# One attention body of a recurrent block: state products in strips, variances in float32r, key gates behind the first values

## The reference

```python
gk = jax.nn.log_sigmoid(xn @ Wkg1 @ Wkg2 + bkg2) / NORMALIZER
v = xn @ Wv
g = xn @ Wg + bg
def step(S, inp):
    qt, kt, vt, gt = inp
    S = S * jnp.exp(gt)[..., None] + kt[..., None] * vt[..., None, :]
    ot = jnp.einsum('bhk,bhkd->bhd', qt, S)
    return (S, ot)
mu = jnp.mean(o, axis=-1, keepdims=True)
var = jnp.var(o, axis=-1, keepdims=True)
o = (o - mu) * jax.lax.rsqrt(var + 1e-05)
o = jax.nn.silu(g) * o
x = x + o @ Wo
```

## Time and profile before

| | us |
|---|---|
| runs: lowest, median, highest | 1624.19, 1628.15, 1628.93 |
| profiled execution: its own time, span | 1622.4, 1620.7 |
| PE busy | 1593.2 (98%) |
| PE weight loads busy | 1277.6 (79%) |
| DVE busy | 847.3 (52%) |
| ACT busy | 567.2 (35%) |
| POOL busy | 167.2 (10%) |

### The profile page before, as it was taken

How to read it: one execution, slowest core, us unless ns; L and a number is a source line. 1 busy time by engine, 2 the same in 40 slices (tenths; PEclk the granted TensorE clock), 3 DMA queues, 4 the chain that set the end, 5 groups by cost and what they waited for, 6 DMA issues and landing times.

```text
span 1620.7 us, 30581 instructions
## 1 busy us (share of the span) xinstructions
PE 1593.2 (98%) x12274; PEld 1277.6 (79%) x12274; DVE 847.3 (52%) x1311; ACT 567.2 (35%) x982; POOL 167.2 (10%) x190
## 2 busy tenths in 40 slices
PE   7999999999999999999999999999999999999998
PEld 5777888777777777777777788888888888888886
DVE  5565455367797887978876451331415142241413
ACT  4333343366564645636564411111111111111111
POOL 4770000100220102101020000000000000000000
PEclk9999999999999999999999999999999999999999
DMA  7563332101020210202213423030301203030200
GB/s 175 151 135 78 83 95 69 59 27 52 9 84 0 84 53 32 84 0 84 84 54 118 144 101 127 0 136 0 136 0 49 87 0 136 0 136 0 91 14 26
DMA packets 50700, 113.16 MB, mean 70 GB/s; under 512 B 13321, under 2 KB 24665, under 8 KB 42466
## 3 DMA queue, kind: packets, MB, share of 16 engines
q1 hardware_dynamic: 47906, 99.95, 19.5%
q10 hardware_dynamic: 1152, 8.39, 1.3%
q0 software_dynamic: 1600, 4.25, 0.9%
HBM read 78.98 MB, written 33.59 MB: 69 GB/s over the span
## 4 chain that ended last, share of the span: by engine, by line
PE 94%; DVE 2%; ACT 1%; issue 1%; DMA 1%; PEld 0%; SPq 0%; ACTq 0%; DVEq 0%; PEldq 0%
PE m_ps L1529 10%; PE m_ps L1531 10%; PE m_ps L1530 10%; PE a_ps L160 7%; PE a_ps L162 7%; PE a_ps L161 7%; PE f_ps L160 5%; PE f_ps L162 5%; PE f_ps L161 5%; PE m_ps L1543 5%; PE m_ps L1544 5%; PE m_ps L1545 5%; PE a_att L1282 3%; PE a_ps L1399 2%; PE a_ps L1303 2%; PE a_ps L1390 1%
## 5 line engine op out<-in xcount | busy, mean ns | idle before, releaser
L1529 PE MATMUL m_ps<-m_xshi,m_w 128*128 128x512 f32 x680 | 268.1, 394 | 1.4 <-DVE m_w L1520 1.4
L1766 DVE TENSOR_TENSOR m_h<-m_ps,m_silu 128x512 f32<-128x512 f32 x85 | 58.7, 690 | 402.4 <-PE m_ps L1531 402.4
L1531 PE MATMUL m_ps<-m_xshi,m_w 128*128 128x512 f32 x680 | 266.5, 392 | 0.0
L1530 PE MATMUL m_ps<-m_xslo,m_w 128*128 128x512 f32 x680 | 266.4, 392 | 0.0
L1830 ACT ACTIVATE m_silu<-m_ps 128x512 f32<-128x512 f32 x85 | 50.8, 597 | 334.3 <-PE m_ps L1531 334.3
L1529 PEld LDWEIGHTS m_ps<-m_xshi,m_w 128*128 128x128 f32 x680 | 127.7, 188 | 30.0 <-issue 2.1
L1531 PEld LDWEIGHTS m_ps<-m_xshi,m_w 128*128 128x128 f32 x680 | 127.6, 188 | 28.7
L1530 PEld LDWEIGHTS m_ps<-m_xslo,m_w 128*128 128x128 f32 x680 | 127.7, 188 | 28.1 <-issue 0.2
L1101 POOL TENSOR_TENSOR row<-row,a_r 128x512 f32<-128x512 f32 x32 | 50.7, 1615 | 331.6 <-DMA a_r<-scratch_r 331.6
L1022 DVE TENSOR_TENSOR a_a<-a_att,causal 128x1024 f32<-128x1024 f32 x64 | 75.2, 1216 | 11.8 <-PE a_att L1282 11.8
L1839 ACT ACTIVATE m_h0hi<-m_h 128x512 fp32r<-128x512 f32 x46 | 29.1, 632 | 135.7 <-DVE m_h L1766 135.7
(11 more groups left out here) (306 smaller groups left out, 3487.9 us busy)
## 6 DMA issues: line engine op xcount, KB each, us to landing
row<-scratch_xn SPq DMA_DIRECT2D x16, 1024.0 KB, 4.9
row<-scratch_xmid SPq DMA_DIRECT2D x16, 1024.0 KB, 7.3
m_xt<-in_L_attn_W SPq DMA_DIRECT2D x33, 256.0 KB, 3.2
f_xt<-in_L_attn_x SPq DMA_DIRECT2D x32, 256.0 KB, 8.1
scratch_xn<-row SPq DMA_DIRECT2D x8, 1024.0 KB, 9.0
scratch_gate<-row ACTq DMA_DIRECT2D x8, 1024.0 KB, 3.9
scratch_xmid<-row SPq DMA_DIRECT2D x8, 1024.0 KB, 3.9
row<-scratch_gate SPq DMA_DIRECT2D x8, 1024.0 KB, 10.5
```

The costliest lines, as they stand in the source:

```text
L1529: pe.matmul(ps, wh, xh, start=k == 0, stop=False)
L1530: pe.matmul(ps, wh, xl, start=False, stop=False)
L1531: ins = pe.matmul(ps, wl, xh, start=False, stop=k == LAST)
L1766: dve.tensor_tensor(h[n], dense.region(f"b{j}"), silu[n], ALU.mult).then_inc(dense.taken_sem(f"b{j}"), 1)
```

## The change

Five edits go together.

1. The state is kept for two heads per strip of 32 partitions (`state`, 64 columns a group instead of 256). The products with the queries become eight strips of 32 rows and 64 columns, and the outputs of a chunk go to two PSUM banks, `ps_mix` EVEN and ODD, half of each.
2. Half of the ODD bank holds the turned keys; when neither is in use the whole of it is the third bank of `dense` (z0, v2, g1, o0, o3). The other results go by turns to the two remaining banks (`places`). v1 and g0 are still neighbours in one bank, as are g0 and g3.
3. ScalarE splits the squares into a high part, VectorE makes the low part (`squares_lo`), and the variance is two float32r products.
4. The inner gate is laid out in four groups of 16 rows, taken out by one copy on ScalarE and one subtraction on VectorE, instead of three copies and a subtraction on VectorE.
5. On TensorE and ScalarE the keys' transposes of chunks 1 and 2 move behind the parts of row i + 1, and z moves behind v0 and the last variance.

```diff
@@ phase_a @@
-        state = [sb(f"state{n}", [P, GR, HG * VH]) for n in range(2)]
+        state = [sb(f"state{n}", [P, GR, 2 * VH]) for n in range(2)]
...
-        psum = [ctx.enter_context(nc.psum_tensor(f"a_ps{b}", [P, 512], F32))[:] for b in range(4)]
+        psum = [ctx.enter_context(nc.psum_tensor(f"a_ps{b}", [P, 512], F32))[:] for b in range(2)]
+        ps_mix = ctx.enter_context(nc.psum_tensor("a_mix", [P, 2, 512], F32))[:]
+        EVEN, ODD = 0, 1
...
+        places = {result: n for n, results in enumerate((
+            ["k0", "ds0", "var0", "q0", "ds2", "var2", "v0", "z1", "v3", "g2", "o1"],
+            ["k1", "u", "ds1", "var1", "q1", "ms", "var3", "v1", "g0", "g3", "o2"],
+            ["z0", "v2", "g1", "o0", "o3"])) for result in results}
...
+        turned = Regions(count, "kt", [ps_mix[:, ODD, GR * P:]], list(range(NC - 1)))
...
@@ vector @@
-                dve.tensor_copy(u[0:RANK], ps).then_inc(count.sem("uhi"), 1)
-                dve.tensor_copy(u[64:64 + RANK], ps).then_inc(count.sem("uhi"), 1)
-                dve.tensor_copy(u[96:96 + RANK], at.region("u")[32:32 + RANK]).then_inc(count.sem("uhi"), 1)
...
+            def squares_lo(i, c):
+                dve.wait_ge(*count.at("sqhi", i, c + 1))
+                dve.tensor_tensor(og_hl[1][:, :, tokens(c)], sq, og_hl[0][:, :, tokens(c)].bitcast(F32),
+                                  ALU.subtract).then_inc(count.sem("sqlo"), 1)
...
@@ scalar, body @@
-                    if c + 1 < NC:
-                        act.wait_ge(*dense.ready(f"kt{c}", i))
-                        act.activation(flat(kt_sb), dense.region(f"kt{c}")[:, 0:GR * P],
-                                                            ACT.Copy).then_inc(dense.taken_sem(f"kt{c}"), 1)
-                    for part in (("k0", "k1"), ("c1",), ("q0",), ("q1",))[c]:
+                    if c == 0:
+                        keys(i, c)
+                    if c == 1:
+                        squares(i, (2,))
+                    for part in (("k0", "k1"), ("u",), ("q0",), ("q1",))[c]:
                         ahead(part)
+                    if 0 < c < NC - 1:
+                        keys(i, c)
...
+                    act.wait_ge(*count.at("sq", i, c + 1))
+                    act.activation(og_hl[0][:, :, tokens(c)], sq, ACT.Copy).then_inc(count.sem("sqhi"), 1)
-                ahead("z")
                 ahead("v0")
                 inverse_deviation(i, NC - 1)
+                ahead("z")
                 ahead("exponentials")
                 ahead("g")
...
@@ tensor @@
-                pe.matmul(ps, avg32, flat(sq), start=True, stop=True).then_inc(dense.ready_sem(f"var{c}"), 1)
+                pe.matmul(ps, avg32r, og_hl[0][:, :, tokens(c)], start=True, stop=False)
+                pe.matmul(ps, avg32r, og_hl[1][:, :, tokens(c)], start=False, stop=True).then_inc(dense.ready_sem(f"var{c}"), 1)
...
-                        for quad in range(QD):
-                            g, first_head = quad * HQ // HG, quad * HQ % HG
-                            pe.matmul(ps[:, quad, :], state[c % 2][:, g, first_head * VH:(first_head + HQ) * VH],
-                                      qhat[:, gcs[g], :], start=quad == 0, stop=True, skip_group_check=True)
+                        for g in range(GR):
+                            for strip in range(4):
+                                rows, at = slice(H32 * strip, H32 * (strip + 1)), H64 * (strip % 2)
+                                pe.matmul(ps[2 * g + strip // 2][at:at + H64], state[c % 2][rows, g, :],
+                                          qhat[rows, gcs[g], :], start=g == 0, stop=True, skip_group_check=True,
+                                          tile_position=(H32 * strip, at))
...
-                ahead("z")
                 ahead("v0")
                 variance(i, NC - 1)
+
+                pe.wait_ge(*mix.taken(NC - 1, i))
+                ahead("z")
                 ahead("v1")
                 ahead("g")
```

More of the change, by code:

```diff
@@ L57, with __init__ @@
 class Regions:
-    def __init__(self, counts, name, regions, order, early=()):
+    def __init__(self, counts, name, regions, order, early=(), places=None):
         self.counts, self.name, self.regions = counts, name, regions
@@ L269, in prepare_attention_weights @@
     step(pool.memset(w["wkg2"].bitcast(F32), 0.0))
-    step(pool.memset(w["wkg1"].bitcast(F32), 0.0))
     RANK, KD = Wkg2.shape
-    small = w["stage"][0:RANK, 1, 0:KD]
+    small = w["stage"][0:4 * RANK, 1, 0:KD]
     sources = {"wkg1": Wkg1, "wk": Wk, "wq": Wq, "wv": Wv, "wg": Wg, "wo": Wo}
@@ L296, in prepare_attention_weights @@
         if name == "wkg1":
-            hi, lo = (w[name][:, kt, at:at + cols] for at in (0, 32))
+            copies = [w[name][:, kt, n * RANK:(n + 1) * RANK] for n in range(4)]
+            for copy in copies[1:3]:
+                step(pool.tensor_copy(copy, s))
+            hi, lo = copies[0], copies[3]
         else:
@@ L843, in phase_a @@
         assert GR == 2 and NC == 4
[L845 to L848, removed]
+        order = [("k0", ["k0"]), ("k1", ["k1"]), (None, ["ds0"]), ("u", ["u"]), (None, ["var0", "ds1"]),
+                 ("q0", ["q0"]), (None, ["var1", "ds2"]), ("q1", ["q1"]), (None, ["var2", "ms"]),
+                 ("v0", values[:1]), (None, ["var3"]), ("z", zs), ("v1", values[1:]), ("g", gates),
                  (None, outs), ("body", [])]
+        places = {result: n for n, results in enumerate((
+            ["k0", "ds0", "var0", "q0", "ds2", "var2", "v0", "z1", "v3", "g2", "o1"],
+            ["k1", "u", "ds1", "var1", "q1", "ms", "var3", "v1", "g0", "g3", "o2"],
+            ["z0", "v2", "g1", "o0", "o3"])) for result in results}
         early = {part: results for part, results in order if part}
-        late = {order[n + 1][0]: results for n, (part, results) in enumerate(order) if not part}
-        dense = Regions(count, "dense", psum[0:3], sum((results for _, results in order), []), sum(early.values(), []))
+        dense = Regions(count, "dense", psum + [ps_mix[:, ODD]], sum((results for _, results in order), []),
+                        sum(early.values(), []), places)
+        turned = Regions(count, "kt", [ps_mix[:, ODD, GR * P:]], list(range(NC - 1)))
         att = Regions(count, "att", ps_att, [f"{c}_{n}" for c in range(NC) for n in range(2)])
-        mix = Regions(count, "mix", psum[3:4], list(range(NC)))
+        mix = Regions(count, "mix", [ps_mix[:, :, 0:QD // 2 * P]], list(range(NC)))
         LAST = KT - 1
+        s_avg = outer.enter_context(nc.semaphore("a_avg"))
         parity, s_parity = sb("parity", [P, 2]), outer.enter_context(nc.semaphore("a_parity"))
@@ L1019, in body @@
                     for n in range(2):
+                        if c > 0 and n == 1:
+                            squares_lo(i, c - 1)
                         dve.wait_ge(*att.ready(f"{c}_{n}", i))
@@ L1379, in body @@
                     pe.wait_ge(*mix.free(c, i))
-                    ps = mix.region(c).rearrange("p (q t) -> p q t", t=P)
+                    ps = [mix.region(c)[:, (EVEN, ODD)[quad % 2], quad // 2 * P:(quad // 2 + 1) * P] for quad in range(QD)]
+                    if 0 < c < NC - 1:
+                        pe.wait_ge(*turned.taken(c, i))
                     if c > 0:
@@ L1433, in tensor @@
             f.tensor(pe, first_row)
-            for part in ("v0", "v1", "g"):
+            parts["v0"](0)
+            pass_over(pe, dense, ["z1"], 0)
+            for m in range(KT):
+                pe.wait_ge(*f.dense.taken(f"u{m}", NB - 1))
+            for part in ("v1", "g"):
                 parts[part](0)
+            pe.wait_ge(s_avg, 1)
             loop_parts(pe, NB, parts, body, skip=front.tensor(pe), first=False)
```

118 lines of the change are left out of this document (65 added, 53 removed).

## The result

The changed kernel takes 1683.88 us (median of four runs, 1682.46 to 1684.81), against 1628.32 for the kernel before on the same chip. That is 55.6 us more, or 1.034 times as long by the two medians; the recorded ratio of the runs is 1.0357, 95% interval 1.0341 to 1.0372. Its profiled execution took 1684.57 us with a span of 1682.8, 62.2 us more than the one before, which lies 5.9 us under the median of its kernel. The forecast was 1651, at most 1664: the direction was right and the size about half.

The account below looks back on a forecast made before the run. TensorE, busy 98% of the span, bounds the kernel. About +3.9 us in each of six steady bodies (+23.4), +5 in body 0 and 0 in body 7 gave +28 on 1622.4: 1651 us, 8 in 10 range 1634 to 1664.

Parts of the forecast that it names:

- the wait and its chain: Before g0: z behind v0 delays absolute values by 3.67 us and v1's copy, so TensorE waits 4.0 us a body.
- M: Moment the last chunk's products of weights and values are done, 599.18 before the change, where the key gate products start.
- the case that the forecast priced at 3.1: Rival at g0: offsets pass ahead of GpSimd's first operation, wait only 3.1 us, 1639 us in all; chance 0.30.
- strips that do not run together: Rival in 24 chunks: strips take 0.98 or 1.96 us instead of 0.49, giving 1663 to 1686 us; chance 0.08.
- Behind it g1 waits for v2's copy and g3 for ScalarE's silu of g0: Output gates after the wait at g0: two further waits that move with the chain, 0.9 us a body together.
- M 1.0 us earlier: Inside the chunks: TensorE savings of 0.63, 0.63 and 0.80 us less 1.1 us of new waits, per body.
- a wait of 0.2 us in chunk 1 for VectorE: Chunk 1: keys' product waits 0.2 us while VectorE empties the inner gate's bank after causal products and squares_lo.
- the 1.1 us of waits that the prediction had in the chunks: New TensorE waits: 0.3 us for keys' copies in chunks 1 and 2 each, 0.2 and 0.3 for banks.
- body 0 and body 7: First and last body: +5 us for body 0; 0 for body 7, its savings of 1.3 eaten by weight copies.
- The forecast's four delays: Body 0: moved sums, scans and offsets fall into GpSimd's 7.87 us; four delays of 1.1 for one, +5 us.

Follow-up runs that it names:

- Experiment 2: Kernel before with only z's products moved behind v0 and the last variance on TensorE and ScalarE: 1677.92 us, 1.0307.
- experiment 5: Changed kernel with GpSimd's scaling of the next row held back until VectorE has computed the offsets: 1672.48 us, 1.0278.
- experiment 6: Changed kernel with fp32 variances, no split of squares: 1676.12 us; also with z ahead of v0: 1632.04 us; also with the old inner gate: 1644.63 us.
- experiment 7: Kernel before with 36 added small block products ahead of the attention weights in the last body alone: 1631.16 us, 1.0028.

## Why the prediction was right or wrong

**Right: the wait and its chain.** z behind v0 moved the absolute values by 3.7 us, v1's bank came late, TensorE stood still before g0 for 3.90 us (forecast 4.0), and GpSimd's scaling met the offsets. Experiment 2 shows that z's place alone does it, experiment 5 that GpSimd has 1.1 us of it. From M to g0 a body lost 16.72 - 12.44 = 4.28, where the forecast had 4.07. In body 1 GpSimd came too late to hold the second offset, and the wait was 2.83: the case that the forecast priced at 3.1. The strips run together, 0.60 us a chunk instead of 0.98 (forecast 0.49), and the rival "strips that do not run together", whose time lay nearest, was wrong in its mechanism.

**Wrong, a missing term: what the idle time does to the clock.** The step "Behind it g1 waits for v2's copy and g3 for ScalarE's silu of g0: together 0.9 us" took the output gate block to run at full speed behind the wait. It ran at 1.2 GHz for its first part: 13.47 us on average over six bodies instead of 11.19, 2.3 us a body where 0.9 stood; the waits of g1 and g3 vanish behind it. Over six bodies that is 13.7 us gross and 8.3 more than forecast. I had read in the profile that the clock was 1.00 before and did not ask what a new idle stretch would do to it. The Trainium skill (TensorE: Matmul & The Clock Gate, HAM oscillation — how this bites in real kernels) describes this pattern, waits that let the clock fall so that the next burst starts slowly, and I did not weigh it.

**Wrong, a term of the sum: M 1.0 us earlier.** From o0 to the next M a body took 43.09 to 43.20 us instead of 42.77: 0.3 to 0.4 later. Without the float32r variances (experiment 6) M does come earlier, by 0.75. Their gain was counted in full, with a wait of 0.2 us in chunk 1 for VectorE. This is the row of their first split of squares, with GpSimd's addition beside it (605.64, 1.29 us):

```profile
605.88 1.60 DVE L1073 TENSOR_TENSOR a_oglo<-a_sq,a_oghi 128x512 fp32r<-128x512 f32 x1
```

```profile
605.64 1.29 POOL L1123 TENSOR_TENSOR a_cum<-a_cum 128x512 f32<-128x512 f32 x1 [0.74 <-ACT a_cum L1210]
```

It takes 0.69 us elsewhere. So the variance waits 0.68, and the state update another 0.54 for the inner gate's bank, that VectorE reaches later by the same delay:

```profile
607.61 0.49 PE L1337 MATMUL a_ps<-a_oghi,a_avg32r 128*128 128x512 f32 x1 [0.68 <-DVE a_oglo L1073]
...
608.27 0.67 PE L1434 MATMUL a_mix<-a_neg,a_state 32*64 32x128 f32 x16
609.47 0.43 PE L1386 MATMUL a_ps<-a_v_tok,a_fold 128*32 128x64 f32 x16 [0.54 <-DVE a_u L948]
```

I had applied the meeting with GpSimd to the offsets and not to the new subtraction. A third wait, 0.31 us for no releaser, stands before the strips of chunk 2 (experiment 6's kernel without the split has none). Of the 1.1 us of waits that the prediction had in the chunks, those for the keys' copies and for q1's bank stand in no steady body; these three, 1.5 us, stand in their place. The gain was also smaller than the sum had it: a product ahead of the strips is dearer, the mean square by 0.2 us and an fp32 variance by 0.1. Experiment 6 puts the float32r variances at +1.3 us a body, 0.5 of it the clock, and +7.8 us in all: the edit meant to save is the second largest loss.

**Wrong: body 0 and body 7.** The forecast had +5 and 0. In the whole, counted between mean square products: up to that of body 0 +6.9 us (3.1 of it before the body starts), to the next +7.7, five steady intervals +33.0, the last interval +12.3, the rest +2.3: 62.2 us. The steady bodies, at 2.7 us above the forecast's 3.9, make 16 of the missing 34. The last body has about 5.7, by its issue waits and the clock; how much of it the strips' instructions make is not shown (experiment 7). Body 0 waits 6.93 us before g0 instead of 0.48, and has issue waits of 1.21, 0.34 and 1.42 us as well: 6.5 us above the forecast. There the scans and a sum lie in GpSimd's scaling (413.55, for 5.80 us), not the offsets, which begin behind it:

```profile
413.11 3.48 DVE L967 TENSOR_TENSOR_SCAN a_cum<-ones,a_neg 128x128 f32<-128x128 f32 x4
416.51 1.72 DVE L963 TENSOR_TENSOR a_neg<-a_neg,a_soft 128x512 f32<-128x512 f32 x1
418.26 2.31 DVE L967 TENSOR_TENSOR_SCAN a_cum<-ones,a_neg 128x128 f32<-128x128 f32 x4
420.61 2.36 DVE L974 TENSOR_TENSOR a_lv<-a_cum 128x1024 f32<-128x1024 f32 x2
```

In a steady body the first three take 1.37, 0.67 and 1.37 us, so the meeting costs 4.1, as the wait does that experiment 5 takes away. The forecast's four delays are right in number, with the offsets wrongly among them; what it left out is the issue waits, 3.0 us together.

**Open.** The 3.1 us before body 0, and perhaps the issue waits in body 0, need not belong to the change. The two profiles of the one-copy gate in the kernel before are of one and the same kernel, and their first key products start at 367.72 and 371.52 us, their first mean square products at 394.74 and 400.24; the second has an issue wait of 1.54 us on the way and the first has none. Over all kernels here the first key product starts between 367.7 and 373.3 us. Why the lower clock lasts for g0 alone in some bodies and longer in the next ones, by turns, no run here tells. That instructions come too slowly where code is run for the first time was not shown beyond the place of the issue waits.

## What to carry to other kernels

A wait that opens on a busy TensorE can cost more than its own length: add what the products behind it take at the lower clock, and ask it of every new idle stretch, short ones too. Before moving a small product behind a large one, follow the longest chain that starts with the small one, since its place was worth more than all savings of the change together. And when a saving on TensorE is bought with an operation on VectorE, look at what GpSimd does at that moment, in each chunk. Last, where two profiles differ by a few microseconds, look at how far two profiles of the same kernel lie apart at the same place.

## What the runs showed of the hardware

- At g0 the granted clock fell to the 1.2 GHz level behind every idle stretch from 3.01 to 7.02 us, behind each of the eight of 2.83 us in steady bodies but not behind the one in body 0 of experiment 5, behind 2.05 us in two of six, and not behind 0.34 to 0.48 us. Products of 512 float32r columns then started 0.43 us apart instead of 0.23, for g0 alone or for longer; a block of 48 such products took 12.7 to 14.1 us instead of 11.19.
- A VectorE subtraction with two operands in the state buffer took 1.60 us beside a GpSimd addition, 0.69 alone: 0.9 us late, more than its whole length. A sum took 1.72 us beside GpSimd's scaling, 0.67 alone. An offset that had begun before the scaling was not held.
- In code that is run for the first time 36 small products, 0.5 us of work by estimate, went with 6.3 us more in the profile of a body, of them 2.4 in issue waits. In the loop's later turns four more per chunk, with the float32r variances, showed one issue wait of 0.3 us a body.
- Eight products of 32 rows and 64 columns in four strips took 0.60 us with 128 moving columns, against 0.98 for four with 128 rows and 128 columns. A fp32 product of 512 columns took 1.04 to 1.06 us (mean square) or 0.96 (variance) ahead of the strips, and 0.86 ahead of the four full products.
- Two profiles of one kernel lay 5.5 us apart at the first mean square product (394.74 and 400.24 us).
